# One projection for a narrow unit's q and k, full-width operands for its preparation and for the transposes of the maxima, and a changed order of steps

## The reference

```python
# _L0_attn_ref: on the left half of the 128 channels only
left = x[..., :E // 2]
q = (left @ Wq.T).reshape(N, S, 16, 4)      # k and v alike
energy = einsum('nqhd,nkhd->nqkh', q, k)
att = softmax(energy / scale, axis=2)
out = einsum('nqkh,nkhd->nqhd', att, v).reshape(N, S, 64)
return out @ Wo.T + bo
# _L0_ffn_ref: attention with 16 heads of 8 and rotary q and k, then a gated mixture of experts
q = src @ Wq; k = src @ Wk_c @ Wk; v = src @ Wv_c @ Wv      # q, k rotated
x = rmsnorm(src + softmax(q k^T / sqrt(8)) v @ Wo, norm1_w)
shared = swiglu(x @ W_shared_in) @ W_shared_out
h = swiglu(x @ W1_shared)
routed = sum over the best 2 of 8 experts (within the better group) of (h @ W2_experts[e]) * w[:, e]
out = rmsnorm(x + shared + routed, norm2_w)
# the whole
x = x + 0.5 * ffn(layernorm(x))
x = x + attn(layernorm(x))
x = x + 0.5 * ffn(layernorm(x))
```

## Time and profile before

| | |
|---|---|
| median of three runs | 844.42 us (844.34 to 846.73) |
| the profiled execution | 846.46 us, of which the span is 844.5 |
| PE busy | 815.6 us, 97% of the span |
| DVE busy | 669.5 us, 79% |
| ACT busy | 504.1 us, 60% |
| POOL busy | 364.5 us, 43% |
| mean granted clock of PE | 0.985 |

### The profile page before, as it was taken

The page is one execution under the profiler, slowest core; times in us unless marked ns, Lnnn a source line. Parts: engine busy times, 40 slices in busy tenths (PEclk is TensorE's granted clock), DMA queues, the critical chain, the costliest instruction groups (busy, mean ns, idle before and its releaser), DMA issues.

```text
span 844.5 us, 13469 instructions
## 1 busy us (share of the span) xinstructions
PE 815.6 (97%) x4431; PEld 310.6 (37%) x4431; DVE 669.5 (79%) x1317; ACT 504.1 (60%) x1077; POOL 364.5 (43%) x762
## 2 busy tenths in 40 slices
PE   8899999999999998999999999999999999999995
PEld 4333344334333342332323232233344334355553
DVE  6889997697679758876889999989987787674266
ACT  3266664475457636755788777767764475475541
POOL 2563427714442364445532735515151734343532
PEclk9799999999999999999999999999999999999998
DMA  3454302110110011020010322303102200000000
GB/s 106 138 138 128 101 5 57 38 58 9 35 38 2 5 41 37 3 64 17 3 49 33 85 73 54 102 2 99 54 11 68 76 2 14 1 4 13 1 14 13
DMA packets 24700, 37.83 MB, mean 45 GB/s; under 512 B 6464, under 2 KB 22080, under 8 KB 23048
## 3 DMA queue, kind: packets, MB, share of 16 engines
q1 hardware_dynamic: 24053, 35.95, 15.0%
q10 hardware_dynamic: 579, 1.03, 0.3%
HBM read 27.03 MB, written 9.11 MB: 43 GB/s over the span
## 4 chain that ended last, share of the span: by engine, by line
PE 80%; DVE 14%; issue 2%; ACT 2%; POOL 2%; DMA 0%; POOLq 0%; ACTq 0%; DVEq 0%
PE ps_out L961 17%; PE ps L900 15%; PE ps L934 13%; PE ps L1035 12%; DVE maxes L1154 9%; PE ps L1020 7%; PE ps L856 3%; PE ps_out L950 2%; PE ps L1027 2%; PE ps L922 2%; PE ps L866 1%; PE ps L998 1%; ACT probs L1359 1%; PE ps L1011 1%; PE ps L986 1%
## 5 line engine op out<-in xcount | busy, mean ns | idle before, releaser
L1359 ACT ACTIVATE probs<-ps 128x512 f32<-128x512 f32 x768 | 414.3, 598 | 225.2 <-PE ps L934 203.7
L1154 DVE TENSOR_REDUCE maxes<-ps 128x1 f32<-128x512 f32 x768 | 479.8, 681 | 53.7 <-PE ps L900 51.5
L900 PE MATMUL ps<-k_aug,q_aug 72*128 72x512 bf16 (+1 forms) x768 | 247.7, 386 | 4.3 <-issue 2.5
L934 PE MATMUL ps<-q_aug,k_aug 75*128 75x512 bf16 (+1 forms) x704 | 231.6, 383 | 2.4 <-DVE maxes L1154 0.9
L961 PE MATMUL ps_out<-probs,v_aug 128*18 128x512 f32 x1408 | 185.6, 599 | 3.0 <-ACT probs L1359 2.1
L900 PEld LDWEIGHTS ps<-k_aug,q_aug 72*128 72x128 bf16 (+1 forms) x768 | 64.9, 97 | 169.2 <-issue 117.0
L1035 PE MATMUL ps<-w,hidden 128*128 128x512 f32 x256 | 118.7, 596 | 0.0
L934 PEld LDWEIGHTS ps<-q_aug,k_aug 75*128 75x128 bf16 (+1 forms) x704 | 59.0, 97 | 131.4 <-issue 83.8
L1251 DVE TENSOR_TENSOR prod<-ps,gate 128x512 f32<-128x512 f32 x56 | 38.7, 691 | 53.6 <-PE ps L1035 43.0
L1471 POOL TENSOR_SCALAR max_parts<-maxes 128x16 bf16<-128x16 f32 (+1 forms) x38 | 11.0, 290 | 141.7 <-DVE maxes L1154 141.5
L1551 POOL TENSOR_TENSOR prod<-prod 128x512 f32<-128x512 f32 x28 | 35.5, 1267 | 76.9 <-DVE prod L1251 57.4
(11 more groups left out here) (159 smaller groups left out, 770.1 us busy)
## 6 DMA issues: line engine op xcount, KB each, us to landing
q_aug<-qk_parts SPq DMA_DIRECT2D x7, 1152.0 KB
k_aug<-qk_parts SPq DMA_DIRECT2D x21, 384.0 KB
qk_parts<-parts SPq DMA_DIRECT2D x48, 128.0 KB, 2.3
q_aug<-qk_parts SPq DMA_DIRECT2D x11, 288.0 KB
k_aug<-qk_parts SPq DMA_DIRECT2D x24, 96.0 KB
qk_parts<-parts SPq DMA_DIRECT2D x24, 64.0 KB, 2.0
X<-in_x_dram SPq DMA_DIRECT2D x4, 256.0 KB, 4.3
w<-in_ffn_W_experts_dram SPq DMA_DIRECT2D x2, 512.0 KB, 4.2
```

The source lines that it names most:

```text
L900: pe.matmul(bank(use[i]), q_aug[p0:p1, r, at, qt * 128:(qt + 1) * 128], k_aug[p0:p1, r, at, :], start=True, stop=True).then_inc(bank_full[ ...
L934: pe.matmul(bank(use[i]), k_aug[p0:p1, r, at, kt * 128:(kt + 1) * 128], q_aug[p0:p1, r, at, :], start=True, stop=True).then_inc(bank_full[ ...
L1154: dve.tensor_reduce(maxes[:, u % 2, qt, at:at + 1], full(use[0]), AX.X, ALU.max).then_inc(bank_free[use[0][0]], 1)
L1359: act.activation(probs[:, step % P_RING, c:c + exp_run(u), :], both(use), ACT.Exp, scale=scale)\
```

## The change

- In a narrow unit one `qk_project` makes q and k together: the weight is awq's first two 64-column blocks side by side, 128 columns; q comes out on partitions 0 to 63 and k on 64 to 127. ACT copies all 128 rows once, POOL splits them once, and both semaphore counts go up by two at a time. SP stores q's three parts and then k's three from the two halves of `parts`, all at the place of the one split.
- `awq` has 128 rows; the lower 64 are set to zero by DVE at the start, and the narrow `x_transpose` turns all 128 columns, ACT copies 128 rows, and `v_project` contracts over 128.
- `max_parts` is 128 columns wide, and every transpose of the maxima turns all of them; ACT still copies only the 48 or 96 rows that mean something.
- The hold of `x_transpose` is 32 instead of 26.
- Places are changed in PREP_2, 5 to 8, 10 and 11, in POST_2 to 5, 8, 9, 11 and 12, in MAX_LATE and in LATE_LOADS. Of unit 3's experts the places go from 44 to 55 to 42 to 67.

```diff
-PREP_2 = {... "qk_project": [23, 34], "qk_split": [29, 49], "v_project": [27], "stack": [47, 73]}
+PREP_2 = {... "qk_project": [23, 34], "qk_split": [29, 52], "v_project": [27], "stack": [50, 76]}
-PREP_5 = {"norm_stats": [9], "norm_apply": [13], "x_transpose": [19], "qk_project": [29, 41], "qk_split": [39, 49],
-          "v_project": [40], "stack": [44, 55]}
-PREP_6 = {"norm_stats": [5], "norm_apply": [10], "x_transpose": [13], "qk_project": [18, 33], "qk_split": [26, 40],
-          "v_project": [16], "stack": [27, 47]}
-PREP_7 = {"norm_stats": [8], "norm_apply": [12], "x_transpose": [20], "qk_project": [21, 35], "qk_split": [28, 44],
-          "v_project": [28], "stack": [43, 59]}
-PREP_8 = {"norm_stats": [-11], "norm_apply": [4], "x_transpose": [4], "qk_project": [24, 36], "qk_split": [25, 40],
-          "v_project": [31], "stack": [35, 51]}
+PREP_5 = {"norm_stats": [9], "norm_apply": [15], "x_transpose": [19], "qk_project": [35, 43], "qk_split": [40, 49],
+          "v_project": [68], "stack": [50, 57]}
+PREP_6 = {"norm_stats": [4], "norm_apply": [9], "x_transpose": [10], "qk_project": [19, 36], "qk_split": [30, 36],
+          "v_project": [14], "stack": [45, 47]}
+PREP_7 = {"norm_stats": [22], "norm_apply": [28], "x_transpose": [33], "qk_project": [39, 47], "qk_split": [40, 48],
+          "v_project": [36], "stack": [42, 61]}
+PREP_8 = {"norm_stats": [-10], "norm_apply": [-1], "x_transpose": [1], "qk_project": [24, 35], "qk_split": [27, 57],
+          "v_project": [31], "stack": [41, 73]}
...
-POST_3 = {"heads_out": [3, 3], "heads_transpose": [4], "out_project": [7], "rms_stats": [12, 63], "rms_apply1": [17],
-          "x1_transpose": [20], "logits": [22], "mlp_up": [27, 27, 30, 34],
-          "router": [24, 24, 25, 29, 39, 42, 43, 45], "shared_out": [38], "expert": [44, 46, 46, 49, 49, 51, 54, 55],
-          "rms_apply2": [67], "ffn_out": [68]}
-POST_4 = {"heads_out": [4, 4], "heads_transpose": [7], "out_project": [16], "attn_out": [31]}
-POST_5 = {"heads_out": [4, 8], "heads_transpose": [11], "out_project": [15], "attn_out": [31]}
+POST_3 = {"heads_out": [3, 3], "heads_transpose": [4], "out_project": [8], "rms_stats": [10, 72], "rms_apply1": [13],
+          "x1_transpose": [20], "logits": [22], "mlp_up": [23, 27, 33, 34],
+          "router": [23, 23, 25, 31, 38, 41, 42, 42], "shared_out": [39], "expert": [42, 47, 50, 55, 59, 62, 66, 67],
+          "rms_apply2": [77], "ffn_out": [77]}
+POST_4 = {"heads_out": [3, 7], "heads_transpose": [11], "out_project": [16], "attn_out": [28]}
+POST_5 = {"heads_out": [3, 3], "heads_transpose": [8], "out_project": [20], "attn_out": [42]}
...
-MAX_LATE = [39, 33, 23, 18, 16, 17, 22, 24, 24, 21, 16, 13, 13]
+MAX_LATE = [39, 33, 23, 18, 10, 18, 22, 24, 24, 17, 17, 13, 14]
...
-HOLD = {"x_transpose": 26,
+HOLD = {"x_transpose": 32,
...
-        max_parts = sb("max_parts", [128, TT * PARTS * HH], BF16)
+        max_parts = sb("max_parts", [128, 128], BF16)
-        awq = sb("awq", [C // 2, 3, C // 2])
+        awq = sb("awq", [C, 3, C // 2])
...
+            elif is_ffn(u):
+                engine.wait_ge(part_done, parts_before(u, qk) + c + 1)
             else:
-                engine.wait_ge(part_done, parts_before(u, qk) + c + 1)
+                engine.wait_ge(part_done, parts_before(u, 0) + 2 * (c + 1))
...
                     store_parts(sp, u, qk)
+                    if not is_ffn(u):
+                        store_parts(sp, u, 1)
...
-                        mm = pe.transpose(o[0:rows, t * 128:(t + 1) * 128], src[:, b, t, 0:rows], ident[:, :])
+                        mm = pe.transpose(o[:, t * 128:(t + 1) * 128], src[:, b, t, :], ident[:, :])
...
-                    pe.matmul(bank(use[0])[0:rows, :], (wq, wk)[qk][:, :] if ffn else awq[:, qk, :], xT[0:rows, :],
+                    pe.matmul(bank(use[0]), (wq, wk)[qk][:, :] if ffn else awq[:, 0:2, :].rearrange("k a m -> k (a m)"), xT[:, :],
                               start=True, stop=True).then_inc(bank_full[use[0][0]], 1)
...
-                    n = TT * PARTS * H // max_pieces(u)
-                    pe.transpose(bank(use[0]).bitcast(BF16)[0:n, 0:128], max_parts[:, 0:n], identb[:, :])\
+                    pe.transpose(bank(use[0]).bitcast(BF16)[:, 0:128], max_parts[:, :], identb[:, :])\
...
+            dve.memset(awq[C // 2:C, :, :], 0.0).then_inc(awq_padded, 1)
...
-                    ins = act.activation(qf[0:rows, :], full(use[0])[0:rows, :], ACT.Copy)
+                    ins = act.activation(qf[:, :], full(use[0]), ACT.Copy)
```

More of the change, by code:

```diff
@@ L225 @@
           "v_project": [63], "stack": [63, 80]}
-PREP_2 = {"norm_stats": [12], "norm_apply": [14], "x_transpose": [21], "qk_project": [23, 34], "qk_split": [29, 49],
-          "v_project": [27], "stack": [47, 73]}
+PREP_2 = {"norm_stats": [12], "norm_apply": [14], "x_transpose": [21], "qk_project": [23, 34], "qk_split": [29, 52],
+          "v_project": [27], "stack": [50, 76]}
 PREP_3 = {"norm_stats": [-2], "norm_apply": [7], "x_transpose": [19], "qk_project": [31, 36], "qk_split": [31, 36],
@@ L280 @@
            "router": [53, 56, 57, 58, 64, 66, 66, 66], "shared_out": [60], "expert": [59, 63, 67, 68],
[L281 to L285, removed]
-MAX_LATE = [39, 33, 23, 18, 16, 17, 22, 24, 24, 21, 16, 13, 13]
+           "expert_add": [66, 66, 68, 73], "finish": [87, 93]}
+POST_12 = {"heads_out": [3], "heads_transpose": [4], "out_project": [5], "rms_stats": [14], "rms_apply1": [16],
+           "x1_transpose": [39], "logits": [43], "mlp_up": [54, 59, 65, 69],
+           "router": [72, 80, 87, 101, 101, 102, 104, 110], "shared_out": [81], "expert": [70, 82, 93, 99],
+           "expert_add": [116, 130, 147, 169], "finish": [171, 177]}
+MAX_LATE = [39, 33, 23, 18, 10, 18, 22, 24, 24, 17, 17, 13, 14]
 ROWS_LATE = 5
@@ L294 @@
 LATE = 19
-LATE_LOADS = [-33, -29, -29, -29, -29, -29, -29, -29, -29, -29, -29, -29, -27, -26, 6, 15, 25, 33, 51]
+LATE_LOADS = [-37, -29, -29, -29, -29, -29, -29, -29, -29, -29, -29, -29, -27, -26, 5, 15, 25, 31, 51]
 def prep_steps(u):
@@ L302, in prep_steps @@
     steps += [(at["qk_project"][0], ("qk_project", u, 0)), (at["qk_split"][0], ("qk_split", u, 0)),
-              (at["v_project"][0], ("v_project", u)),
-              (at["qk_project"][1], ("qk_project", u, 1)), (at["qk_split"][1], ("qk_split", u, 1))]
+              (at["v_project"][0], ("v_project", u))]
+    if is_ffn(u):
+        steps += [(at["qk_project"][1], ("qk_project", u, 1)), (at["qk_split"][1], ("qk_split", u, 1))]
     if u == 0:
@@ L332, in post_steps @@
     return steps + stats[1:] + [(at["rms_apply2"][0], ("rms_apply2", u)), (at["ffn_out"][0], ("unit_out", u))]
-HOLD = {"x_transpose": 26, "qk_project": 31, "v_project": 32, "heads_transpose": 23, "out_project": 32,
+HOLD = {"x_transpose": 32, "qk_project": 31, "v_project": 32, "heads_transpose": 23, "out_project": 32,
         "x1_transpose": 32, "logits": 32, "shared_out": 38, "expert": 33, "max_rows": 26, "heads_out": 27,
@@ L515, in macaron @@
         blank_set = sem("blank_set")
+        awq_padded = sem("awq_padded")
         wq_turned = sem("wq_turned")
@@ L560, in macaron @@
             (wo[:, :], w["ffn_Wo"]),
-            (awq[:, 2, :], w["attn_WvT"]),
+            (awq[0:C // 2, 2, :], w["attn_WvT"]),
             (awo[:, :], w["attn_WoT"]),
@@ L572, in macaron @@
             for g in range(2):
-                late.append((awq[:, i, g * 32:(g + 1) * 32].rearrange("p (i d) -> p i d", i=4), of[:, g, :, :]))
+                late.append((awq[0:C // 2, i, g * 32:(g + 1) * 32].rearrange("p (i d) -> p i d", i=4), of[:, g, :, :]))
         large = len(late)
@@ L643, in parts_before, with both_parts, part_of @@
             return PARTS * (2 * u + qk - 2)
+        def both_parts(u):
+            return 1 if is_ffn(u) else 2
+        def part_of(u, qk, c):
+            if is_ffn(u):
+                return parts[:, qk, c, :]
+            return parts[qk * C // 2:(qk + 1) * C // 2, 0, c, :]
         def part_ready(engine, u, qk, c):
@@ L664, in split @@
         def split(eng, seq, own_wait, u, qk):
-            rows = H * head_dim(u)
-            rest, _, q = (x[0:rows, :] for x in rotated(u, qk))
+            rest, _, q = rotated(u, qk)
             taken(eng, "qk_project", u, qk)
@@ L679, in split @@
                 eng.wait_ge(parts_stored[qk], PARTS * 16 * (u - qk))
-            h, m, l = (parts[0:rows, qk, c, :] for c in range(PARTS))
-            n, done = parts_before(u, qk), part_done
-            eng.tensor_copy(h, q).then_inc(done, 1)
-            eng.wait_ge(done, n + 1)
+                if qk == 0 and not is_ffn(u - 1):
+                    eng.wait_ge(parts_stored[1], PARTS * 16 * (u - 1))
+            h, m, l = (parts[:, qk, c, :] for c in range(PARTS))
+            n, done, two = parts_before(u, qk), part_done, both_parts(u)
+            eng.tensor_copy(h, q).then_inc(done, two)
+            eng.wait_ge(done, n + two)
             seq(eng.tensor_tensor(rest, q, h, ALU.subtract))
```

(10 more changed lines are left out.)

24 lines of the change are left out of this document (13 added, 11 removed).

## The result

The kernel after takes 837.03 us (median of four runs, 836.87 to 837.55); the kernel before, beside it, 844.78. The ratio is 0.9904, with a 95% interval of 0.989 to 0.9919: 7.7 us less. Run again beside other executions of the kernel before, the same kernel came to 837.93 against 844.93, ratio 0.9916 (0.9901 to 0.993). The forecast was 838.1, 6.3 less; by its interval the measured gain is 6.8 to 9.3 us.

A forecast was written before the change was run, and what follows sets the result against it. PE was taken to bound the kernel, except units 4 to 7, where PE and DVE take turns. Terms 4.1 + 2.0 + 0.2 + 0.5 + 0.7 + 0 - 1.2 = 6.3 us off 844.42 gave 838.1, range 832.5 to 843.5.

The forecast's parts named there:

- The projections: Narrow units 4 to 7: one q and k projection instead of two saves 1.3, 1.2, 1.1 and 0.5, together 4.1 us.
- v (0.2): Unit 4's v product, 128 rows instead of 64: a step fewer at each side, 0.2 us saved.
- The transposes: Transposes of the maxima in seven units, 128 columns instead of 48: smaller steps beside full-array work, 2.0 us saved.
- (a): Unit 5's v product moves from unit 3's PE-bound stretch to where PE idles in unit 4's: 0.5 us saved.
- (b): Unit 3's last two experts move from unit 4's stretch into unit 5's: 1.7 us gained to 1.2 lost, 0.7 gained taken.
- (c): Unit 4's maxima begin six places earlier, shifting some of unit 3's maxima between PE-bound stretches: 0.
- (d): Unit 9's maxima begin at place 17 instead of 21, so unit 8's run denser in unit 7's stretch: 1.2 us lost.
- The signs: Stretches: units 3 and 4 each fall about 3 us, unit 7 grows 1 to 2, others move under 1.
- DVE takes it back: Units 4 to 7 are DVE's alone, so savings and moves there bring nothing: 842.1 us, chance 0.19.
- The moves fill the holes: Moved work halves PE's idle time and low-clock loss in units 4 to 6: 4 us more, 834; chance 0.14.
- Transposes without gain: The step around the maxima's transposes comes from something other than width: 840.1 us, chance 0.06.
- Late k rows: Unit 8's later k load, margin 1.3 us, stops PE if late: 840 to 849.6 us, chance 0.09.

The follow-up runs named there:

- experiment 1: Kernel after with all places, MAX_LATE, LATE_LOADS and the hold of x_transpose as in the kernel before: 838.88 us against 845.31, ratio 0.9919.
- experiment 3: Kernel before with only max_parts made 128 columns wide and all 128 transposed: 843.16 us, ratio 0.9974.
- experiment 7: Kernel after with unit 5's v product back at place 40 instead of 68: 839.30 us, ratio 0.9923.
- experiment 5: Kernel after with unit 3's experts back at their old places, 44 to 55: 838.65 us, ratio 0.9916.
- experiment 9: Kernel after with unit 4's first maximum at place 16 again instead of 10: 838.49 us, ratio 0.9916.
- experiment 8: Kernel after with unit 9's first maximum at place 21 again instead of 17: 836.01 us, ratio 0.9888.
- experiment 2: Kernel before with all places, MAX_LATE, LATE_LOADS and the hold of x_transpose of the kernel after: 842.77 us, ratio 0.9966.
- experiment 12: Kernel after run again unchanged, beside other executions of the kernel before: 837.93 us, ratio 0.9916.
- experiment 10: Kernel after with unit 8's k split at place 64 instead of 57 and its k load at 80 instead of 73: 843.98 us, ratio 0.9988.
- experiment 11: Kernel before with the maxima's transposes 64 columns wide instead of 48 in units of four pieces: 845.0 us, run once.

## Why the prediction was right, point by point

The time lies 1.1 us under the forecast and within its range. The profiled execution took 837.1, 3.1 us less than the 840.2 reckoned for it.

- **The projections (4.1) and v (0.2).** Right in size: with the transposes they make 6.3 in the sum and 6.4 in experiment 1; by the rest of the span they are 3.8 of the 4.3 (experiment 1 less experiment 3). Inside it unit 7's half came to 0.1 instead of 0.5, because unit 5's stretch is DVE's, and the padding adds less than the number of products: 3.9 us come without it (3.5 by the rest of the span). Unit 7's stretch pays 0.4 that the sum did not have.
- **The transposes (2.0).** Right within what can be told: 2.15 in experiment 3, of which 1.3 are seen from unit 1 on and the rest lies in unit 0 and the start-up, where it can't be told from their spread. The mechanism is shown, with the two distances read from the row of 96 columns (0.22 and 0.05, measured 0.22 and 0.06).
- **(a) Unit 5's v product (0.5).** Under-sized; 1.0 by the stretches (experiment 7). The hole was found, but I took half where all of it fits ahead of one wait.
- **(b) The experts (0.7).** Under-sized; 2.0 (experiment 5), and the working was wrong at its root. The two late steps hold PE for 3.7 us and not 1.7, since a float32 product is two records of 0.43 us and each step is two products. Unit 4's stretch gained 4.8 and unit 5's paid 2.8, and neither the 1.7 gained nor the 1.2 lost of the prediction describes them. That the 2.0 lies near the upper bound of 1.7 is chance.
- **(c) Unit 4's earlier maxima (0).** Wrong: 1.7 by the stretches (experiment 9). I looked at PE alone and called it a shift between two PE-bound stretches. Unit 2's stretch pays 0.9 for it, but unit 3's gains 1.7 and unit 4's 0.9; with the later start DVE is 1.4 us busier in unit 3's stretch than after (56.88 against 55.51), and it has to do that beside the RMS products and statistics. That this is why is argued, not shown.
- **(d) Unit 8's denser maxima (-1.2).** Right: 0.8 to 0.9 lost by the stretches (experiment 8).
- **Left out.** The new places lengthen unit 9's stretch by 1.4 and shorten unit 10's by 2.0 (experiment 2 has the same 1.4 and 1.7). Unit 9's own later maxima would make its stretch 0.6 longer still (experiment 8), so the other moves cost 2.0 there. No experiment took these apart.
- **The clock in unit 4's stretch.** Before and in experiment 1 it is 0.98, with every change of places 1.00. Neither the v product, nor the experts, nor unit 4's maxima alone bring the dip back. Which of the other moves removes it stays open.
- **The sum.** The terms for the places (0.5 + 0.7 + 0 - 1.2 = 0) measure 1.0 + 2.0 + 1.7 - 0.9 = 3.8 by the stretches, and all places together 2.5 in experiment 2 (2.2 by the rest of the span). The other moves took more than a microsecond back; against experiment 1, unit 6's stretch is 0.5 longer and unit 9's 1.4, unit 10's 1.6 shorter. So the mechanism of the sum is right for the code, and for the order it is too low in three of four terms. That the time came within 1.1 us of the forecast is in part luck: the terms that were too small stood against costs that had been left out.
- **The signs.** Unit 3's stretch fell by 2.6 (about 3 was said) and unit 7's grew by 1.4 (1 to 2). Unit 4's fell by 8.2 instead of about 3, and units 5, 9 and 10 moved by 3.8, 1.4 and 2.0 where under 1 was said. These misses show the wrong size of (b) and the terms left out, which the total hides. The start-up moved by 0.9, which executions of one kernel do too.
- **Rivals.** *DVE takes it back* falls as a whole (842.1) and holds for unit 5's stretch. *The moves fill the holes* is partly what happened, at 837 and not 834: PE's idle time in units 4 to 6 went from 8.6 to 6.9 us, and the dip of the clock went with it. *Transposes without gain* falls. *Late k rows* didn't occur by a hair: I reckoned the load's issue at 53.8 us into unit 6's stretch, its landing at 62.8 and the first maximum at 64.1. After, the issue is at 53.9, the landing at 64.7 and the maximum at the same 64.7:

```profile
492.65 8.66 DMA k_aug<-ones_row
501.30 0.05 issue
501.35 0.61 PE ps L920 x2
```

These are three links of the chain of waits after. From the issue to the landing it took 10.9 us where I had 9.0, and the first maximum came 0.6 later than reckoned, so the margin of 1.3 us was zero in this execution. In the repeat it was about a microsecond (experiment 12), so it varies with the load. Experiment 10 shows what lies behind it.

## What to carry to other kernels

Before shortening work on the busiest engine, cut the span into stretches and ask of each which engine is idle: the same product cost 1.0 us in one stretch and nothing 30 us later, ahead of a wait that was there anyway. A product that uses part of the array costs more than its columns say when its neighbours use all of it; padding it to the neighbours' shape can be worth more than the work it adds. When a load is moved later to make room, work out on its own queue what it then stands behind, since a few places can decide between nothing and 6 us. And when a row shows a float32 product as two records, price a step by its start to the next start: half a product was enough to make the term of the experts wrong.

## What the hardware showed that I had not expected

- A half-width transpose pays the step of 0.09 us on entering and 0.12 on leaving in bf16 (experiment 11) and pays neither in float32 (rows 7). The Trainium skill (TensorEngine Tiling (Array Packing), Restrictions) says that column tiling disables the transpose mode for float32 input, which would fit: such a transpose then stays in the full mode. No run here separates that from other causes.
- A float32 product of 64 rows and 128 columns takes longer among full-array scores (1.05 us) than one padded with zeros to 128 rows (0.86), though both stream 512 columns twice.
- The same kernel's start-up differs by 1.0 us between two executions with the granted clock at 0.84 and 0.88, and everything after unit 0 repeats within 0.1 us. In the traces of the code of after unit 0 differs too, from 52.3 to 53.6 us, with its granted clock from 1.00 down to 0.98: in the traces kept, the spread is made in the first 95 us.
